# Attention denominators of a head pair in one product of four 32-column tiles, and the output products moved ahead of the value products

## The reference, cut to what matters

```
h   = layernorm(x) * (1 + ca) + sa                 # conditioned by c
x   = x + ga * attention(h)                        # 16 heads of 64, latents of 64, rotary q and k
h   = layernorm(x) * (1 + cb) + sb
x   = x + gb * experts(h)                          # 8 experts, the best by score, relu

attention: scores = q @ k.T / 8 ; attn = softmax(scores, -1)
           out    = (attn @ v) @ w_out.T + residual
```

## Time and profile before

| | us |
|---|---|
| median of three runs | 930.24 |
| profiled execution, its own time | 933.47 |
| its span, first to last instruction | 931.7 |
| TensorE busy | 830.1 |
| VectorE busy | 654.2 |
| GpSimd busy | 660.9 |
| ScalarE busy | 389.1 |
| mean granted TensorE clock | 0.94 |

### The profile page before, as it was taken

The page is one execution under the profiler, slowest core; times in us unless marked ns, Lnnn a source line. Parts: engine busy times, 40 slices in busy tenths (PEclk is TensorE's granted clock), DMA queues, the critical chain, the costliest instruction groups (busy, mean ns, idle before and its releaser), DMA issues.

```text
span 931.7 us, 14679 instructions
## 1 busy us (share of the span) xinstructions
PE 830.1 (89%) x5118; PEld 494.6 (53%) x5118; DVE 654.2 (70%) x1172; ACT 389.1 (42%) x628; POOL 660.9 (71%) x346
## 2 busy tenths in 40 slices
PE   5767989999999999999999999999999977869671
PEld 3434445555555555555555555555555434368571
DVE  7778788667777777777777777777776767545112
ACT  3334344444444444444444444444444423336330
POOL 1488796667978787878787877878778856633323
PEclk8769899999999999999999999999999988979786
DMA  8200001001011010101010111010110000077773
GB/s 205 60 7 7 12 12 24 13 1 26 11 33 22 18 24 13 24 13 24 13 25 13 24 13 24 13 25 13 14 22 13 14 12 1 23 252 257 237 240 87
DMA packets 84330, 43.91 MB, mean 47 GB/s; under 512 B 57632, under 2 KB 73376, under 8 KB 84192
## 3 DMA queue, kind: packets, MB, share of 16 engines
q1 hardware_dynamic: 83232, 40.86, 17.4%
q0 software_dynamic: 1024, 2.10, 0.7%
HBM read 36.51 MB, written 6.16 MB: 46 GB/s over the span
## 4 chain that ended last, share of the span: by engine, by line
PE 74%; DVE 12%; issue 5%; POOL 4%; DMA 2%; ACT 1%; SPq 1%; POOLq 0%; DVEq 0%; ACTq 0%
PE ps_o L446 23%; PE ps_m L412 8%; PE ps_x L400 8%; PE ps_s L430 6%; PE ps_s L432 6%; PE ps_s L436 6%; PE ps_s L434 5%; PE ps_s L463 3%; DVE mx L1063 3%; PE ps_s L454 3%; PE ps_s L576 2%; PE ps_s L585 1%; DMA moe<-xs_dram 1%; DVE hn L1170 1%; POOL xs_dram L920 1%
## 5 line engine op out<-in xcount | busy, mean ns | idle before, releaser
L906 POOL TENSOR_TENSOR acc<-acc,probs 128x1024 f32<-128x1024 f32 (+1 forms) x192 | 459.1, 2391 | 88.1 <-ACT probs L671 66.5
L1063 DVE TENSOR_REDUCE mx<-ps_m 128x2 f32<-128x1024 f32 x240 | 293.7, 1224 | 93.6 <-PE ps_m L412 93.2
L671 ACT ACTIVATE probs<-ps_s 128x1024 f32<-128x1024 f32 x256 | 249.5, 1024 | 156.9 <-PE ps_s L436 156.2
L446 PE MATMUL ps_o<-probs,c_all 128*64 128x512 f32 x1024 | 251.7, 613 | 0.0
L412 PE MATMUL ps_m<-k_hi,q_hi 64*128 64x512 f32 x480 | 109.7, 452 | 20.0 <-DVE mx L1063 19.5
L906 POOL TENSOR_TENSOR acc<-probs 128x1024 f32<-128x1024 f32 (+1 forms) x32 | 75.6, 2362 | 63.5 <-ACT probs L671 63.2
L430 PE MATMUL ps_s<-q_hi,k_hi 64*128 64x512 f32 x512 | 104.2, 403 | 12.0 <-DVE x_sb L1110 10.9
L446 PEld LDWEIGHTS ps_o<-probs,c_all 128*64 128x64 f32 x1024 | 62.8, 137 | 94.5 <-issue 48.2
L412 PEld LDWEIGHTS ps_m<-k_hi,q_hi 64*128 64x128 f32 x480 | 46.6, 185 | 110.2 <-issue 98.7
L432 PE MATMUL ps_s<-q_hi,k_lo 64*128 64x512 f32 x512 | 102.3, 395 | 0.0
L436 PE MATMUL ps_s<-neg_row,one_row 64*128 64x512 f32 x512 | 101.7, 393 | 0.0
(11 more groups left out here) (275 smaller groups left out, 1046.8 us busy)
## 6 DMA issues: line engine op xcount, KB each, us to landing
probs<-in_experts SPq DMA_DIRECT2D x15, 578.0 KB
rr<-rd_dram SPq DMA_DIRECT2D x62, 128.0 KB
wu<-in_wqk SPq DMA_DIRECT2D x16, 256.0 KB, 3.2
neg_row<-nm SPq DMA_DIRECT2D x256, 0.5 KB, 2.0
w_first<-in_experts SPq DMA_DIRECT2D x5, 578.0 KB
rot<-in_experts SPq DMA_DIRECT2D x5, 578.0 KB
hT<-in_experts SPq DMA_DIRECT2D x5, 578.0 KB
xs_dram<-zero SPq DMA_DIRECT2D x2, 960.0 KB, 6.1
```

The lines of the kernel that those rows point to most:

```text
L446: ins = nc.tensor.matmul(ps_o[64 * h:64 * h + 64, :], c_all[:, (p // HP) * TB + kt, :], probs[:, st % 4, h, :], start=(kt == 0), stop=(kt ...
L671: nc.scalar.activation(probs[:, st % 4, :, :], ps_s[:, 2 * (st % 2):2 * (st % 2) + 2, :], ACT.Exp, scale=SCALE).then_inc(s["probs"], 1)
L906: V.tensor_tensor(acc[:, half, heads, :], first, probs[:, st % 4, heads, :], ALU.add).then_inc(s["added"], 1)
L1063: V.reduce_max(mx[:, :, kh, qt], max_banks(q, n), AX.X).then_inc(s["max_reduced"], 1)
```

## The change

The denominators of both halves of a pair come from one call, four products of 32 columns, each on 32 partitions of bank 0: `denominators(p-1, (0, 1), ps_s[:, 0, :])` in group 3 of pair `p`. It and the outputs now stand behind `up` and ahead of the group's value products: outputs of half 0 in group 7, those of half 1 in group 1 of the pair after (`outputs(p-2, 1)`), both into bank 0. They wait for the probabilities of step 2g, no longer for those of step 2g+1. Since the sums live longer, `acc` and `ou` have three buffers. ScalarE copies the denominators at the end of group 3; SyncE has four DMAs in `den_cols` and four in `inv_spread` behind `max_rows(p+1, 0)`; VectorE inverts once per pair, at the start of group 5, divides at the end of groups 6 and 0, and adds the outputs at the end of groups 7 and 1. `score` waits for `out_added` at steps 0 and 4 and for `den_read` at step 8. The last pair keeps two products of 64 columns for half 1, and `outputs(14, 1)` and its division and addition move behind the last pair's loop.

```diff
-        acc = sb("acc", [P, 2, 2, HALF])
+        acc = sb("acc", [P, 3, 2, HALF])
-        ou = sb("ou", [P, 2, HALF])
+        ou = sb("ou", [P, 3, HALF])
...
+        def n_den(p, half=0):
+            return p + 1 + (half if p == LAST else 0)
+        def buf(p, half):
+            return (2 * p + half) % 3
+        def quarter(j):
+            return slice(32 * j, 32 * j + 32)
...
-                if kt == 1:
-                    ge(pe, s["den_read"], n_part(p, half) - 2)
-                    ge(pe, s["out_added"], n_part(p, half) - 3)
+                if st == 0:
+                    ge(pe, s["out_added"], 2 * p - 3)
+                if st == 4:
+                    ge(pe, s["out_added"], 2 * p - 2)
+                if st == TB:
+                    ge(pe, s["den_read"], n_den(p - 1))
...
-            def denominators(p, half, bank):
-                wait_adds(pe, p, TB * half + TB - 1)
-                for h in range(2):
-                    ins = nc.tensor.matmul(bank[64 * h:64 * h + 64, :], ones[:], acc[:, half, h, :], start=True, stop=True)
+            def denominators(p, halves, bank):
+                for half in halves:
+                    wait_adds(pe, p, TB * half + TB - 1)
+                    for h in range(2):
+                        ins = nc.tensor.matmul(bank[quarter(2 * half + h), :], ones[:, 0:32], acc[:, buf(p, half), h, :],
+                                               start=True, stop=True)
...
                     if p + 2 <= LAST:
                         up(p + 2, g)
+                    if p > 0 and g in (3, 7):
+                        pe.wait_ge(s["probs"], n_step(p, 2 * g))
+                        if g == 3:
+                            denominators(p - 1, (0, 1), ps_s[:, 0, :])
+                        else:
+                            outputs(p - 1, 0, ps_s[:, 0, :])
+                    if p > 1 and g == 1:
+                        pe.wait_ge(s["probs"], n_step(p, 2 * g))
+                        outputs(p - 2, 1, ps_s[:, 0, :])
+                    if g == 5 and p == LAST:
+                        denominators(p, (0,), ps_x[:])
                     for n in (2 * g - 2, 2 * g - 1):
...
-                    if g in (3, 7):
-                        pe.wait_ge(s["probs"], n_step(p, 2 * g + 1))
-                    if g == 3 and p > 0:
-                        denominators(p - 1, 1, ps_s[:, 2, :])
-                    if g == 7 and p < LAST:
-                        denominators(p, 0, ps_s[:, 2, :])
-                    if g == 5 and p == LAST:
-                        denominators(p, 0, ps_x[:])
-                    if g == 3 and p > 0:
-                        outputs(p - 1, 0, ps_s[:, 3, :])
-                    if g == 7 and p > 0:
-                        outputs(p - 1, 1, ps_s[:, 3, :])
...
+            last_denominators(ps_x[:])
+            outputs(LAST - 1, 1, ps_s[:, 0, :])
...
-                    if g == 0 and p > 0:
-                        den_out(p - 1, 0, ps_s[:, 2, :])
-                    if g == 4 and p > 0:
-                        den_out(p - 1, 1, ps_s[:, 2, :])
                     expo(p, 2 * g)
                     expo(p, 2 * g + 1)
+                    if g == 3 and p > 0:
+                        den_out(p - 1, ps_s[:, 0, :])
...
-                    if g == 0 and p >= 2:
-                        out_add(p - 2, 1, ps_s[:, 3, :])
-                    if g == 4 and p >= 1:
-                        out_add(p - 1, 0, ps_s[:, 3, :])
+                    if g == 5 and p > 0:
+                        recip(p - 1)
                     if p < LAST:
                         reduce_max(p + 1, 2 * g)
...
                     if p > 0:
-                        if g in (0, 4):
-                            recip(p - 1, g // 4)
-                        if g in (2, 6):
-                            divide(p - 1, g // 4)
+                        if g == 6:
+                            divide(p - 1, 0)
+                        if g == 7:
+                            out_add(p - 1, 0, ps_s[:, 0, :])
+                    if p > 1:
+                        if g == 0:
+                            divide(p - 2, 1)
+                        if g == 1:
+                            out_add(p - 2, 1, ps_s[:, 0, :])
...
             p = LAST
-            out_add(p - 1, 1, ps_s[:, 3, :])
+            divide(p - 1, 1)
+            out_add(p - 1, 1, ps_s[:, 0, :])
             divide(p, 0)
...
+            def den_cols(p, halves):
+                sp.wait_ge(s["den_read"], n_den(p))
+                ge(sp, s["inverses"], p)
+                for half in halves:
+                    for h in range(2):
+                        j = 32 * (2 * half + h)
+                        sp.dma_start(denc[:, half, h, :], den[j:j + 1, :]).then_inc(den_cols_in, 16)
...
                 if p > 0:
-                    if p < LAST + 1:
-                        max_rows(p, 1)
-                    den_cols(p - 1, 0)
-                    inv_rows(p - 1, 0)
-                    inv_spread(p - 1, 0)
+                    max_rows(p, 1)
                 if p < LAST:
                     max_rows(p + 1, 0)
                 if p > 0:
-                    den_cols(p - 1, 1)
-                    inv_rows(p - 1, 1)
-                    inv_spread(p - 1, 1)
+                    den_cols(p - 1, (0, 1))
+                    inv_rows(p - 1, (0, 1))
+                    inv_spread(p - 1, (0, 1))
```

More of the change, by code:

```diff
@@ L208, in build @@
             "added_last": "the same for head 1 of the last pair's second half (vector)",
-            "den_product": "half a pair's denominators (tensor)",
-            "den_read": "and read (scalar)",
-            "inverses": "denominators inverted (vector)",
+            "den_product": "a pair's denominators; half of the last pair's (tensor)",
+            "den_read": "and read (scalar, the last half vector)",
+            "inverses": "and inverted (vector)",
             "sums_copied": "latent sums of half a pair are in SBUF (scalar)",
@@ L448, in pv, with last_denominators @@
                 ins.then_inc(s["sums"], 1)
-            def denominators(p, half, bank):
-                wait_adds(pe, p, TB * half + TB - 1)
+            def denominators(p, halves, bank):
[4 more added lines that the diff above has]
+                                               start=True, stop=True)
+                ins.then_inc(s["den_product"], 1)
+            def last_denominators(bank):
+                wait_adds(pe, LAST, NSTEP - 1)
                 for h in range(2):
-                    ins = nc.tensor.matmul(bank[64 * h:64 * h + 64, :], ones[:], acc[:, half, h, :], start=True, stop=True)
+                    ins = nc.tensor.matmul(bank[64 * h:64 * h + 64, :], ones[:], acc[:, buf(LAST, 1), h, :],
+                                           start=True, stop=True)
                 ins.then_inc(s["den_product"], 1)
@@ L675, in o_out, with den_out @@
                 act.wait_ge(s["sums"], NSTEP * p + TB * half + TB)
[L677 to L682, removed]
+                ge(act, s["out_product"], n_part(p, half) - 3)
+                nc.scalar.copy(ou[:, buf(p, half), :], ps_o[:]).then_inc(s["sums_copied"], 1)
+            def den_out(p, bank):
+                act.wait_ge(s["den_product"], n_den(p))
+                ge(act, den_cols_in, 64 * p)
                 nc.scalar.copy(den[:], bank).then_inc(s["den_read"], 1)
@@ L900, in add @@
                     first = probs[:, (st - 1) % 4, heads, :]
-                    ge(pool, s["den_product"], n_part(p, half) - 2)
+                    ge(pool, s["den_product"], n_den(p + half - 2))
                 else:
-                    first = acc[:, half, heads, :]
+                    first = acc[:, buf(p, half), heads, :]
                     pool.wait_ge(s["added"], n_add(p, st) - 1)
-                V.tensor_tensor(acc[:, half, heads, :], first, probs[:, st % 4, heads, :], ALU.add).then_inc(s["added"], 1)
+                V.tensor_tensor(acc[:, buf(p, half), heads, :], first, probs[:, st % 4, heads, :], ALU.add).then_inc(s["added"], 1)
             def inverse_root(b):
@@ L1144, in add_head1 @@
                     first = probs[:, (st - 1) % 4, 1, :]
-                    dve.wait_ge(s["den_product"], n_part(LAST, half) - 2)
+                    dve.wait_ge(s["den_product"], n_den(LAST - 1))
                 else:
-                    first = acc[:, half, 1, :]
+                    first = acc[:, buf(LAST, half), 1, :]
                     dve.wait_ge(s["added_last"], n_add_last(st) - 1)
-                V.tensor_tensor(acc[:, half, 1, :], first, probs[:, st % 4, 1, :], ALU.add).then_inc(s["added_last"], 1)
+                V.tensor_tensor(acc[:, buf(LAST, half), 1, :], first, probs[:, st % 4, 1, :], ALU.add).then_inc(s["added_last"], 1)
             def block_stats(tiles):
```

59 lines of the change are left out of this document (29 added, 30 removed).

## The result

The kernel after takes **939.4 us** (median of 4 runs, 938.5 to 943.1) where the kernel before takes 929.6 beside it (927.5 to 930.4): ratio 1.0125, 95% interval 1.0101 to 1.0149. In a later series of runs it was 939.8 against 929.2, ratio 1.0106 (1.0078 to 1.0134). The change made the kernel slower by about 10 us; forecast were 928.0 and a range that ends at 940.

A forecast was written before the change was run, and what follows sets the result against it. TensorE's work was taken to bound the kernel until something else is late. Terms -0.9 - 3.5 - 1.1 - 1.7 + 11 x 1.0 - 0.4 - 5, unrounded -2.0, against 930.2 gave 928 us, range 915 to 940.

The forecast's parts named there:

- pair 1: Start of the kernel: less work, group 2's division stall and an old wait gone, a new wait added; -3.5 us in all.
- pair 2: Start of the kernel: extra work in this pair covers both new waits, so -1.1 us.
- pair 3: A division hit in group 2, a wait of 1.61, goes: -1.7 us, beside the steady +1.0.
- pair 14: Next-to-last pair: its groups lack `up`, its two divisions hit additions before and after; -0.4 us.
- the end: Pair 15: `score` no longer waits for `out_add` behind VectorE's routing work; -5 us, bounds -1 and -8.
- TensorE's work: Per steady pair, four-tile denominators 1.06 and outputs 0.88 each: 2.82 after instead of 3.86, 1.04 us less.
- The wait at the inversion: Group 5: inversion at +12.81 from group 3's start delays the reduction; TensorE waits 1.3, 1.4 with a slower first product.
- The division in group 0: Division moved there waits for GpSimd's addition, ends near +6.1, delaying group 1's second maxima: 0.5, 0.6 with slow first product.
- the steady pairs' term: Eleven equal pairs: 44.13 - 1.04 + 1.4 + 0.6 = 45.1, one microsecond longer each, 11 x 1.0.
- The second wait: Pair 15's wait of 5.62 for `out_add`: moves to `counts_before`, some 4 us earlier in VectorE's list.
- the first wait: Pair 15's wait of 5.30 for `out_add`: only moves to `h2_features`, which needs the same normalisation; -1.
- The slow-side rival: Group 6's division misses its gap between GpSimd's additions: 1.9 with following delay, 21 in 11 pairs, 949 us; chance 0.08.

The follow-up runs named there:

- third profile of the kernel before: The kernel before, unchanged, run once more in the third series for its profile: 930.6 us, span 928.9, without the stall in the expert stage.
- second: The kernel after, unchanged, run once more in the second series with a second profiled execution: 939.8 us, ratio 1.0106 to the kernel before.
- the doubled one: Four-tile product issued twice: in the kernel after 939.5 us, ratio 1.0126; in the kernel with all three edits 920.2 us, ratio 0.9901.
- the first mend: The kernel after with den_cols(p-1) ahead of max_rows(p+1, 0) on SyncE, nothing else changed: 945.9 us, ratio 1.0112 to the kernel before.

## Why the prediction was wrong

The kernel after against the third profile of the kernel before, stage by stage, in us:

| stage | forecast | first profile after | second |
|---|---|---|---|
| ahead of pair 0 | 0 | +0.3 | -0.4 |
| pair 0 | -0.9 | -0.8 | -0.5 |
| pair 1 | -3.5 | +0.6 | -1.1 |
| pair 2 | -1.1 | +1.2 | +0.3 |
| pair 3 | -0.7 | -2.5 | -2.5 |
| pairs 4 to 13 | +9.6 | +11.5 | +15.2 |
| pair 14 | -0.4 | +1.3 | -0.3 |
| pair 15 to the end | -5 | -3.6 | -2.3 |
| sum | -2.0 | +7.9 | +8.5 |

The steps that failed, by what each missed in the two profiles: pair 1 (4.1 and 2.4), pairs 4 to 13 (1.9 and 5.6), pair 2 (2.3 and 1.4), the end (1.4 and 2.7), pair 14 (1.7 and 0.1). Pair 3 missed by 1.8 the other way.

- **TensorE's work, right.** Forecast were 1.06 for the four-tile product and 0.88 for outputs behind `up`; groups 3 and 7 exceed a plain one by 1.0 and 0.90. Column tiles of 32 run four abreast. The product alone is 0.87 (the doubled one), so the changes of tile around it cost 0.13, where 0.2 was forecast for them. The outputs, forecast at 1.07 behind 64-column tiles and 0.88 behind tiles of their own shape, have 0.90 there. The Trainium skill (TensorEngine Tiling (Array Packing), Key Properties) says that changing the tiling mode drains the engine; the outputs agree, since behind `up` the mode stays and the difference of 0.17 is gone.
- **The wait at the inversion, right.** +12.81 forecast, +12.79 measured; TensorE's wait is 1.2, and group 5 is 1.5 longer than a plain one, where 1.4 was forecast. That it makes the product's cost irrelevant was right too (the doubled product).
- **The division in group 0, right.** End at + 6.1 forecast, 413.76 - 407.69 = + 6.07 measured, 0.60 a pair. A steady pair was forecast at 45.1 and is 45.07 to 45.28 where no DMA takes 1.0 or more to issue. That it fits to 0.02 is in part luck: the saved work is 0.1 more than forecast and the wait 0.1 more, and they cancel.
- **Failed: the steady pairs' term, taken as equal eleven times.** Of the 220 DMAs of rows and columns in pairs 3 to 13, three or four take 1.0 to 1.5 us to issue instead of 0.6, and the kernel before has as many, three in each profile. Before they were hidden. After, the chain is on the path, and I left its variance out: +1.9 in one profile, +5.6 in the other, where it also brought the clock down. In the first profile the pairs with such a column DMA (5, 8 and 12) are each 0.5 longer, as their inversions are later. The earlier trace rows are one such chain, in which no DMA is late, and I priced all eleven by it.
- **Failed: pair 1.** I credited it 3.5 for work and two stalls. In group 2 VectorE waits for GpSimd, whose list sets the pace there by the trace, so all that TensorE saved ahead turned into waiting: 3.1 instead of 1.9. Behind that wait the clock fell (0.72 or 0.83 over the group, 1.00 before), which cost another 1.5 to 2.8: the group's length less 5.03, less the wait, and less the 0.3 that is left over in the kernel before too. A row of the kernel before hints at it, the first two groups of pair 1, and I hadn't asked for it. GpSimd is busy 9.90 of 10.33 us:

```profile
116.40:126.73 10.33, 10.33 (x66) 5.71 (x64) 8.23 (x16) 5.77 (x9) 9.90 (x5) 1.00 0.11 15
```

- **Failed: pair 2.** I said its extra work covers both waits. `out_add` now stands behind `second_batch`, which waits for TensorE: 2.2 at `score`, shown by moving it (2.3 back in group 1). I had looked at this step only in steady groups.
- **Mis-sized: the end.** -5 was the middle of two bounds; -2.3 and -3.6 came. The second wait did shrink (group 4 of pair 15 from 13.3 to 9.7 and 9.5), but group 0 grew by 1.3 to 1.5 and group 1 by 1.0, since the first wait moved to `h2_features` and there is 6.6 instead of 5.3.
- **Pair 3** went better than forecast: behind the wait of 1.61 of the earlier trace rows, the clock fell in the two later profiles of the kernel before (group 3 of 10.5 instead of 8.9), and that went with the wait. The forecast rests on the first profile, where it hadn't, so 1.6 of this is the base and no merit of the change. **Pair 14** is the reverse: a wait of 1.68 in both profiles after, with the clock fallen in the first.
- **The slow-side rival** (group 6) didn't strike after the change. It was the next in line behind the wait of group 5, though, and took back all that the first mend won. I had weighed it as an alternative to the wait, not as what the wait covers. I had priced it at 1.9 a pair; it came out at 2.2 or 3.8.

The medians differ by 9.8 and 10.6, the profiles by 7.9 and 8.5. That is the profiled executions: the third of the kernel before took 1.5 more than the median beside it, the two of the kernel after 0.9 and 0.6 less than theirs.

## What to carry to other kernels

When two small steps are merged into one, their results come later and their consumers don't move: follow the merged data through every queue (here twelve DMAs on one queue ahead of the inversion), and reorder the queue with the change; here that, with two moves on VectorE, turned +10 us into -21. A wait that repeats in every iteration may be the cover of the next one, so mend and look again until the bound engine is busy throughout. Price a chain of DMAs with its late ones, not with its median, as soon as it stands on the path.

## What the runs showed of the hardware

- A stall of VectorE and ScalarE in the expert stage, with waits of 4.0 to 6.7 us for which the profile names no releaser of this core, stood in 4 of 4 traces on one chip and in 0 of 8 on two others; two more traces, one with it and one without, have no chip on record. It made the last stretch of the kernel before 4.8 and 5.6 us longer, and its median on that chip was 5.6 us higher.
- TensorE's granted clock fell behind every single wait of 3.1 us, ten of ten (the eight value products behind it took 2.6 to 3.7 us instead of 1.94, with 0.73 to 0.50 of the clock granted; 0.50 is the lower of its two levels throughout), behind some of those between 1.6 and 2.2 (3.15 behind one of 1.61 and 3.17 behind 1.92, but an unchanged 1.94 behind waits of 1.94, 1.96 and 2.15), and behind none of the many of 1.2 to 1.4. A wait of 1.6 to 2.2 cost its own length, or that and 1.3 to 1.6 more.
- VectorE operations that take 0.17 and 0.68 us alone took 0.8 to 2.9 where they met a GpSimd addition, until that one ended. Little decides whether they meet: in group 6 a division at S6 + 4.53 took 0.68, one at S6 + 4.89 took 2.84.
